# RWKV block with expert gathers: a quarter of the gate and up blocks moved beside the first two expert tiles, down projection two tiles behind, x normed again per tile

## What is computed

```python
xn = layernorm(x)
# recurrent part: xk, xv, xr are mixes of xn and xn shifted by one token
k, v, sr = xk @ Wk.T, xv @ Wv.T, sigmoid(xr @ Wr.T)
s = (sr * wkv(-exp(time_decay), time_first, k, v)) @ Wo.T
# experts: 4 heads, 8 of 16384 experts each, so 32 rows per token
q = xn @ Wq.T;  indices, scores = product_key_top8(q, keys)
w = silu(einsum(xn, down_embed[indices])) * softmax(scores)
experts = einsum(w, up_embed[indices])
# dense part, 4096 wide
mlp = (silu(xn @ Wg.T) * (xn @ Wu.T)) @ Wd.T
out = x + s * silu(mlp + experts)
```

## Time and profile before

| what | us |
|---|---|
| median of 3 runs (slowest core) | 2036.66 |
| lowest and highest of the 3 | 2027.74, 2050.11 |
| the profiled execution | 2017.81 |
| its span, first to last instruction, slowest core | 2016.3 |
| PE, DVE, ACT, POOL busy in it | 1346.1, 1239.5, 901.7, 854.6 |

### The profile page before, as it was taken

The page is one execution under the profiler, slowest core; times in us unless marked ns, Lnnn a source line. Parts: engine busy times, 40 slices in busy tenths (PEclk is TensorE's granted clock), DMA queues, the critical chain, the costliest instruction groups (busy, mean ns, idle before and its releaser), DMA issues.

```text
span 2016.3 us, 23266 instructions; the slowest of 8 cores (1998.7 to 2016.3 us)
## 1 busy us (share of the span) xinstructions
PE 1346.1 (67%) x5504; PEld 553.6 (27%) x5504; DVE 1239.5 (61%) x2515; ACT 901.7 (45%) x1480; POOL 854.6 (42%) x776
## 2 busy tenths in 40 slices
PE   0168876988778777888522665666665666765678
PEld 0133332433233333333200222222222222222233
DVE  3646888478766887577522655555565565655554
ACT  3544323443244432535255744545454555544543
POOL 0033334333343333430222655656555655655561
PEclk9989987998889887999755888888888888888887
DMA  8899999999999999993799999999999999999995
GB/s 263 284 291 318 316 316 315 326 309 320 312 317 312 320 309 315 320 305 106 226 319 333 300 326 324 331 320 329 321 325 325 330 327 326 328 321 325 325 325 166
DMA packets 233718, 616.32 MB, mean 306 GB/s; under 512 B 38384, under 2 KB 71152, under 8 KB 231536
## 3 DMA queue, kind: packets, MB, share of 16 engines
q1 hardware_dynamic: 95616, 276.87, 41.8%
q0 software_dynamic: 73888, 268.73, 41.6%
q10 hardware_dynamic: 64080, 69.24, 11.8%
HBM read 514.35 MB, written 100.66 MB: 305 GB/s over the span
## 4 chain that ended last, share of the span: by engine, by line
DMA 36%; PE 25%; DVE 19%; issue 10%; ACT 5%; POOL 3%; DVEq 1%; SPq 0%; ACTq 0%; POOLq 0%
DMA arena<-tabb,expi 28%; PE ps_c L400 6%; PE ps_b L400 6%; PE ps_d L400 4%; DMA arena<-x_nat 3%; DVE arena L587 3%; DMA arena<-wdT 3%; PE ps_a L400 3%; POOL arena L383 3%; DVE arena L643 2%; DVE arena L641 2%; DVE arena L647 2%; ACT arena L1021 2%; PE ps_d L529 1%; PE ps_a L529 1%
## 5 line engine op out<-in xcount | busy, mean ns | idle before, releaser
L383 POOL DMA_INDIRECT arena<-tabb,expi x512 | 552.5, 1079 | 535.8 <-PE ps_a L529 197.4
L1021 ACT ACTIVATE arena<-arena 128x1024 bf16<-128x1024 bf16 x384 | 404.5, 1054 | 429.5 <-DVE arena L849 424.8
L369 POOL CAST arena<-arena 128x1024 bf16<-128x1024 f32 x256 | 300.3, 1173 | 594.2 <-DMA arena<-downE 339.1
L849 DVE TENSOR_TENSOR arena<-arena 128x1024 bf16<-128x1024 bf16 x384 | 263.2, 692 | 381.8 <-DMA arena<-tabb,expi 287.7
L400 PE MATMUL ps_b<-arena 128*128 128x512 bf16 x1024 | 263.8, 403 | 68.9 <-ACT arena L950 68.9
L400 PE MATMUL ps_c<-arena 128*128 128x512 bf16 x1024 | 258.7, 397 | 17.3 <-DVE arena L766 17.3
L529 PE MATMUL ps_a<-arena 128*128 128x512 bf16 x384 | 129.6, 498 | 198.5 <-DVE arena L819 198.5
L766 DVE TENSOR_TENSOR arena<-arena,ps_c 128x512 bf16<-128x512 bf16 x128 | 84.6, 681 | 186.9 <-PE ps_c L400 107.9
L400 PE MATMUL ps_a<-arena 128*128 128x512 bf16 x512 | 138.4, 420 | 69.7 <-ACT efac L933 46.9
L842 DVE SCALAR_TENSOR_TENSOR arena<-arena 128x1024 bf16<-128x1024 bf16 x128 | 156.5, 1223 | 34.0 <-DMA arena<-tabb,expi 27.7
L950 ACT ACTIVATE arena<-ps_b 128x512 bf16<-128x512 f32 x128 | 73.0, 596 | 214.8 <-PE ps_b L400 199.2
(11 more groups left out here) (97 smaller groups left out, 1582.5 us busy)
## 6 DMA issues: line engine op xcount, KB each, us to landing
arena<-downE SPq DMA_DIRECT2D x128, 512.0 KB, 10.2
arena<-upE SPq DMA_DIRECT2D x128, 512.0 KB, 10.3
tabb<-arena SPq DMA_DIRECT2D x256, 256.0 KB, 8.6
arena<-x_nat SPq DMA_DIRECT2D x32, 512.0 KB, 11.0
arena<-wgS ACTq DMA_DIRECT2D x32, 512.0 KB, 12.0
arena<-wuS ACTq DMA_DIRECT2D x32, 512.0 KB, 10.0
h_scr<-arena ACTq DMA_DIRECT2D x64, 256.0 KB, 12.2
arena<-h_scr SPq DMA_DIRECT2D x16, 1024.0 KB, 10.8
```

What stands on the lines that cost most here:

```text
L369: e.tensor_copy(out=tout[s], in_=ring[s]).then_inc(pool_cast, 1)
L383: e.indirect_dma_start(out=gslot[n % NSLOT], out_offset=None, in_=d_tabb, in_offset=IndirectOffsetOnAxis(ap=expi[:, n:n + 1], axis=0)).the ...
L849: e.tensor_tensor(out=pdot[q % 3], in0=gslot[slot][:, 0:1024], in1=xnl[w % 2], op=ALU.mult).then_inc(dv_prod, 1)
L1021: e.activation(out=pdot[q % 3], in_=pdot[q % 3], func=AF.Copy, accum_out=dots[:, g * GS + x:g * GS + x + 1]).then_inc(ac_dots, 1)
```

## The change

- `items(u)`: even units run one item, odd units two, so 48 of the 64 items stand beside the units. The last 16 (pairs 12 to 15) stand beside the groups of expert tiles 0 and 1, one item a group (`tail_item`).
- `quantum`: the down projection of tile t stands beside tile t + 2. Tiles 14 and 15 take two tiles each. `finished(w, g)` says where a tile's last step stands.
- xn is not stored to DRAM nor loaded again. `norm_again(t)` makes it on VectorE from x, which is loaded anyway for the residual, into one of 4 buffers instead of 2.
- Of the 40 weight chunks 16 are loaded and cast in tile 0 (two a group), 24 in tile 2 (four a group), because the hidden state's inputs occupy their place until tile 1 ends.
- 16 gather slots instead of 18.
- Constants of the arena move, and the keys lie in it.

```diff
-NSLOT = 18
+NSLOT = 16
+NI1 = 48
+    def items(u):
+        return range(u * 3 // 2, (u + 1) * 3 // 2)
+    def tail_item(w, g):
+        return NI1 + w * NG + g
     def quantum(w, g):
-        if w == 0:
+        if w < 2:
             return []
-        if w < NT - 1:
+        if w == 2:
+            lo = (0, 2, 6, 10, 14, 20, 26, 32, 32)
+            return [(0, range(lo[g], lo[g + 1]), range(KC) if g == 7 else ())]
+        if w < NT - 2:
             lo = (0, 5, 10, 16, 21, 26, 32, 32, 32)
-            if g < 6:
-                return [(w - 1, range(lo[g], lo[g + 1]), ())]
-            return [(w - 1, (), range(4 * (g - 6), 4 * (g - 5)))]
+            return [(w - 2, range(lo[g], lo[g + 1]), range(4 * (g - 4), 4 * (g - 3)) if g in (4, 5) else ())]
+        t = 2 * w - NT
...
# sync_prog
-            e.dma_start(out=d_xn[ts(t), :], in_=xnt[t % 2]).then_inc(st_xn[t % 2], 16)
+        for i in range(2):
+            e.wait_ge(st_rw[i], 16 * 16)
+        load_xt(0)
+        load_xt(1)
+        load_xt(2)
+        for c in range(16):
+            load_wd(c)
+        load_xt(3)
+        e.wait_ge(pe_u, 4 * NIC)
+        e.wait_ge(dv_h1, 4 * NIC)
+        e.wait_ge(ac_gu, 2 * NIC)
+        for i in range(2):
+            e.wait_ge(st_h1[i], 16 * 32)
+        load_h1(0)
+        for c in range(16, 20):
+            load_wd(c)
...
# tensor_prog, units
-            gu_unit(2 * u, 0)
-            gu_unit(2 * u, 1)
+            its = items(u)
+            gu_unit(its[0], 0)
+            if m % 2:
+                gu_unit(its[0], 1)
...
-            gu_unit(2 * u + 1, 0)
+            if m % 2:
+                gu_unit(its[1], 0)
             if u + 1 < NU:
                 v_unit(u + 1)
-            gu_unit(2 * u + 1, 1)
+            gu_unit(its[-1], 1)
# tensor_prog, expert tiles
             for g in range(NG):
+                if w < 2:
+                    gu_unit(tail_item(w, g), 0)
+                    gu_unit(tail_item(w, g), 1)
# vector_prog, expert tiles
+        def norm_again(t):
+            e.wait_ge(ld_xt[t % 4], 16 * (t // 4 + 1))
...
+            e.tensor_scalar(out=xnl[t % 2], in0=xt[t % 4], scalar1=mv[:, 2 * t:2 * t + 1],
+                            scalar2=rstd[:, t:t + 1], op0=ALU.subtract, op1=ALU.mult).then_inc(dv_xnl, 1)
+                if w < 2 and g:
+                    hidden(2 * tail_item(w, g - 1))
+                    hidden(2 * tail_item(w, g - 1) + 1)
                 if g:
                     weigh(w, g - 1)
...
+                if g == 6 and w + 1 < NT:
+                    norm_again(w + 1)
# scalar_prog, expert tiles, after the Silu of the group's weights
-                if w == 0:
-                    for c in range(5 * g, 5 * g + 5):
+                if w < 2:
+                    it = tail_item(w, g)
+                    if 4 + it < 2 * NIC:
+                        cast_gu(4 + it)
+                    gate(2 * it)
+                    store_h1(it - 1)
+                    gate(2 * it + 1)
+                    if w == 0:
+                        cast_d(2 * g)
+                        cast_d(2 * g + 1)
+                elif w == 2 and g < 6:
+                    if g == 0:
+                        store_h1(2 * NIC - 1)
+                    for c in range(16 + 4 * g, 20 + 4 * g):
+                        cast_d(c)
```

More of the change, by code:

```diff
@@ L25 @@
 NEXP = 16384
-XS = T + 4
+XS = T + 2
 NU = NB * KC
@@ L44 @@
 A_XN = A_WQ + 8192
-A_E = A_XN + KC * XS * 2
+A_GUS = A_XN + KC * XS * 2
+A_WST = A_GUS
+A_GU = A_WST + 8192
+A_SG = A_GU + 16384
+A_H1S = A_SG + 2048
+A_E = A_H1S + 4096
 A_ZB = A_E
@@ L49 @@
 A_SR = A_DEN + 2048
[L50 to L54, removed]
+A_Q = A_SR + 8192
 A_RWS = A_Q + 4096
 A_TK = A_RWS + 2048
-A_END1 = A_TK + 5120
+A_KEYS = A_TK + 5120
 B_SLOT = 0
+B_PD = B_SLOT + NSLOT * 4096
+B_DG = B_PD + 3 * 2048
 B_WD0 = A_MIX
+B_WO = A_E
+B_XT = B_WO + 16384
+B_XNL = B_XT + 16384
 B_WD1 = A_XN
[L62 to L70, removed]
+B_H1T = A_GUS
+B_RWT = B_H1T + 16384
+B_OT = B_RWT + 4096
+A_END = max(A_KEYS + 2048, B_XNL + 4096)
 def ts(i, n=128):
@@ L181, in build @@
     rwt = [b16(B_RWT + i * 2048, 1024) for i in range(2)]
-    xt = [f32(B_XT + i * 4096, 1024) for i in range(2)]
+    xt = [f32(B_XT + i * 4096, 1024) for i in range(4)]
     ot = [f32(B_OT + i * 4096, 1024) for i in range(2)]
-    dst_ = [f32(B_XT + i * 4096, 1024) for i in range(4)]
+    wd_st = [f32(B_WO + i * 4096, 1024) for i in range(4)]
     pdot = [b16(B_PD + i * 2048, 1024) for i in range(3)]
@@ L783, in vector_prog @@
             step_o(u)
-            hidden(4 * u)
-            hidden(4 * u + 1)
+            its = items(u)
+            hidden(2 * its[0])
             if m % 2:
+                hidden(2 * its[0] + 1)
                 next(pairs)
+                hidden(2 * its[1])
+                next(pairs)
+                if b + 1 < NB and m == 3:
+                    mix(mix_r, 16, b + 1, dv_mixr)
             else:
                 best_keys(t)
-            hidden(4 * u + 2)
-            if m % 2:
-                next(pairs)
-            if b + 1 < NB and m == 3:
-                mix(mix_r, 16, b + 1, dv_mixr)
-            hidden(4 * u + 3)
+            hidden(2 * its[-1] + 1)
             if m % 2:
@@ L988, in scalar_prog @@
                     e.activation(out=q_b[j], in_=ps_x[j % 2], func=AF.Copy).then_inc(ac_q, 1)
-            gate(4 * u)
-            gate(4 * u + 1)
-            if 2 * u + 5 < 2 * NIC:
-                cast_gu(2 * u + 5)
-            gate(4 * u + 2)
-            store_h1(2 * u)
-            gate(4 * u + 3)
+            for i in items(u):
+                if i != items(u)[0]:
+                    cast_gu(4 + i)
+                gate(2 * i)
+                if i:
+                    store_h1(i - 1)
+                gate(2 * i + 1)
         soft(NB - 1)
-        store_h1(2 * NU - 1)
         store_rw(NU - 1)
@@ L1012, in scalar_prog @@
                 i = w * NG + g
-                if g == 0 and w >= 2:
-                    final(w - 2)
-                if g == 5 and w == NT - 1:
-                    final(w - 1)
+                if finished(w, g) is not None:
+                    final(finished(w, g))
                 for x in range(1, GS):
```

140 lines of the change are left out of this document (78 added, 62 removed).

## The result

The change is slightly slower: median 2047.3 us against 2036.3 us over 20 runs each, ratio 1.0062 with a 95% interval of 1.0042 to 1.0082. On a second chip the same change gave 1.007 (1.0046 to 1.0094). I had forecast 2021 us, a gain of 0.8%; 2047 lies inside the range that I gave (1988 to 2054), on the wrong side of no change. The profiled execution of the change has a span of 2047.8 us and that of before 2016.3: 31 us, where the medians differ by 11.

A forecast was written before the change was run, and what follows sets the result against it. Bytes were taken to bound both phases, time being lost only where DMA engines idle. Up to slot reuse -79 us, from there +63, together -16: median 2036.7 to 2021 us, 0.8% less, range 1988 to 2054.

The forecast's parts named there:

- Part 1: From the start to the reuse of gather slots: sixteen items leave the units, -79 us, reuse at about 929.
- m = 0: Four rounds beside the units, TensorE busy 38.3 of 41.6 us: each gains nearly all, 6.5 us, together 26.
- m = 2 and 4: Eight even rounds of 20.0 and 19.5 us: VectorE becomes the bound, each gains 3.3 us, together 26.
- m = 6: Three even rounds of 34.4 us ahead of the last round: 28 to 29 after, each gains 5.5, together 16.
- odd rounds: Fifteen rounds that keep all their work while TensorE comes to them earlier: 0.8 us gained each, together 12.
- The table: First-phase table stream: 13.6 MB leave, counted as 30 us; last cast falls to about 866, so it does not stop the gain.
- Part 2: From the reuse of slots to the end: more bytes and added idle time, +63 us.
- The term of bytes: From slot reuse to the end: 325 MB instead of 319, +6 MB, +19 us at 325 GB/s.
- Tile 1: TensorE's groups of 11.4 us at clock 0.90 make 91 us against 65 of bytes: DMA engines idle 26 us.
- Tile 2: At its head the down projection waits for the load of h, +10 us; the rest bound by bytes, about 100 us.
- The serial chain of VectorE: Rival for the rounds: even rounds lose only their two `hidden`, 22 us, so 2079 us in all; chance 0.12.
- The lower clock: Rival for tiles 0 and 1: TensorE falls to its lower clock, two tiles +124, 2145 us; chance 0.06.

## Why the prediction was wrong

**Part 1, forecast -79 us, measured -50** (reuse of slots at 957.6 against 1007.7; on the second chip 963 against 1001.7, -39; in the mean of the cores -41 and -47). That is outside the bounds of -95 to -60. By its own terms, over the rounds of units 0 to 29, which fell from 820 to 780 us (second chip in brackets, 815 to 782):
- m = 0: forecast -26, measured -14 (-7). TensorE was to give nearly all its 6.9 us a round; the round gave 3.6 (1.7). Mis-sized: TensorE has less to do and waits more for ScalarE ahead of the r and q products, 18.8 us in the four such stretches against 7.1 before (21.4 against 5.9). One of them before, and then with the change:

```profile
589.92 19.14 PE L400 MATMUL ps_d<-arena 128*128 128x512 bf16 x80 [2.20 <-ACT arena L983]
```

```profile
550.10 19.43 PE L436 MATMUL ps_d<-arena 128*128 128x512 bf16 x80 [6.19 <-ACT arena L1036]
```

- m = 2 and 4: forecast -26, measured -40 (-40). VectorE does become the bound, at 16 us.
- m = 6: forecast -16, measured -22 (-15).
- odd rounds: forecast -12, **measured +36** (386 to 422 us; second chip +29). This is the step that failed. "Odd rounds keep all their work; TensorE comes to them earlier" is true of the work, but I had read the move of the items only as instructions on TensorE and VectorE. The store of h is an instruction of ScalarE that moved too, behind the next item's gate, and its landing of 12 us is what frees the buffer. Nearly half of the even rounds' gain was given back in the odd rounds. With the store in its old place slots are reused at 932, which is 70 us before the 1001.7 of that chip (74 in the mean of the cores), where 79 were forecast. That this comes near is partly luck: the odd rounds then stand at +2 where -12 was forecast, m = 0 at -4 where -26 was, and m = 2 and 4 and the next point, which the sum had smaller or not at all, made up for it.
- ahead of the rounds a gain of 11 us was not in the sum at all (the first shared mark, the maximum over k of unit 1, starts at 117.5 instead of 128.5). It comes with the xn stores gone: without the spill alone it starts at 116.6. But there the last mark (unit 31) came at 937.4, where 16 slots with the spill have 937.2, so the early start did not last to the end of the rounds; whether it does in the change is not shown.

One of my own signs of being wrong came true: the rounds shortened by 10.7 us per eight (8.7 on the second chip), less than the 11 that I had set. The table was mis-sized too: its last cast came 44 and 51 us earlier (means of the cores), not 30. So the hole that this part was to close stayed as long as it was, since the units, and not the table, still came last.

**Part 2, forecast +63, measured +82, and +50 on the second chip** (2021.4 - 963.0 against 2010.6 - 1001.7). The first is inside the stated bounds of 52 to 85, the second just outside. The difference between the two is mostly the rate of the executions: tiles 3 to 13 took 17 us more than before on the first chip and 11 us less on the second, while tiles 0 to 2 took 69 and 66 us more. The term of bytes was right: 298 GB/s for 1090 us are 325 MB. Tile 1 was forecast at 91 us with the chain of 1.8 us. It took 82, as the clock was granted at 0.99 and not 0.90. The chain was there, 1.88 us of waiting in a group, and could be removed. Its DMA share of 0.7 was as forecast. Tile 0, at 99 us and a share of 0.93, was inside its range in length and a little under it in share. Tile 2 was forecast at over 105 with a hole at its head, and took 116: the wait for h was 17 us, and the casts' waits for their loads, which I had put under the bytes, were not: VectorE stood up to 22 us behind ScalarE's sums. Slots and `norm_again` cost nothing measurable.

**The rivals.** The serial chain of VectorE (part 1 at -21) is as near to the measured -50 as the forecast, and nearer to the -39 of the second chip, but not by its mechanism: the even rounds, of which it spoke, gave 76 us (62 on the second chip), where it allowed 22. The lower clock did not come (0.90 to 0.99 in tiles 0 and 1). That the norm on VectorE holds up GpSimd's gathers shows no price here: they take 1085 ns in the mean against 1079 before, and the kernel with the norm and without the spill is 0.8% quicker. The stated range was also narrower than its own parts: -95 + 52 and -60 + 85 with 10 us of scatter give 1984 to 2072.

In sum: leaving out the spill gained 0.8% (0.9922). The whole change gained 39 to 50 us ahead of the reuse of slots and lost 50 to 82 behind it (1.0062). With the store issued early it stands at 0.9954, so moving the blocks no longer costs anything that can be told from the spill's gain, but shows no gain of its own either. With the diagonal first (0.983) it does pay: that interval lies clear below the one without the spill alone.

## What to carry to other kernels

When work is moved, follow every instruction that it issues, DMAs first. A store that frees a buffer is on the path as soon as its landing time (12 us here) is longer than the distance to the next writer, and two items in one round bring that writer nearer. In a group whose last product frees a resource (here the up product frees gather slots), put what releases it ahead of work that nobody waits for: 1.9 us of waiting in each group of tile 1 stood there for two products that had time. When a profile says that an engine waits for a DMA, ask first where that DMA is issued, and only then how fast it moves. And look at the other cores before reading a cause off the slowest one: the hole that seemed closed, and the tile that seemed held up by stores, were seen on one or two cores of eight.

## What was not expected of the hardware

Without the 4.2 MB of xn stores the table's last cast came 26 us earlier on the slowest core (860.2 against 886.1 with 16 slots and spill) and 20 us in the mean of the cores, more than the 13 us that those bytes take at 320 GB/s. The third of the page's forty slices ran at 321 GB/s, where that of the kernel before on the same chip has 294. The stores had stood in SP's row between the loads; that this row, and not bytes, sets the start of the first phase was not tried.

In one execution two of the eight cores ran tile 1 at a granted clock of 0.80 with TensorE never idle, while six had 69 us for the same tile; the two lost 15 us by it, about as much as the diagonal gains.

Two chips differ by 1.3% for the same kernel before (2036 and 2010 us), more than the change does; the ratio of the change agrees on them to 0.1% (1.0062 and 1.007).
